# An audio-tower layer on one core: everything outside the attention loop re-laid with features on partitions and tokens on the free axis

## What is computed

```python
# 1. token mixing, x is [8, 4, 750]
a = x^T W1 + b1
for _ in range(8):
    up   = relu(a + shift_r(up)   @ W2.T + b2)
    down = relu(a + shift_l(down) @ W2.T + b2)
h = relu(x^T W3 + b3 + (shift_r(up) @ W4.T + b4) + (shift_l(down) @ W4.T + b4))
# 2. attention with L1 scores, 8 heads, x = layernorm(h)
q, vf, vb = split(x @ wqv.T + bias)
k = x * wk                                   # per head
a = softmax(-sum_w |q - k| / 8)              # with one more zero row
o = sum_heads(a applied to vf + a^T applied to vb)
h = h + x + (o * sigmoid(1.702 o)) @ fanin.T + fanin_b
# 3. mixture of 8 experts, the best 2 by score, x = layernorm(h)
share = softmax over the top 2 of (x @ Wg.T + bg), zero elsewhere
h = h + sum_e share_e * (relu(x @ W1_e.T + b1_e) @ W2_e.T + b2_e)
```

## Time and profile before

| | us |
|---|---|
| median of 3 runs | 9099.83 |
| lowest, highest | 9087.98, 9101.53 |
| the profiled execution | 9099.23 |
| its span, first to last instruction | 9097.4 |
| busy in it: PE, ACT, DVE, POOL | 8899.6, 7702.7, 7116.9, 96.7 |
| mean granted TensorE clock, share of full speed | 0.981 |

### The profile page before, as it was taken

The page is one execution under the profiler, slowest core; times in us unless marked ns, Lnnn a source line. Parts: engine busy times, 40 slices in busy tenths (PEclk is TensorE's granted clock), DMA queues, the critical chain, the costliest instruction groups (busy, mean ns, idle before and its releaser), DMA issues. The chain is left out here.

```text
span 9097.4 us, 256713 instructions
## 1 busy us (share of the span) xinstructions
PE 8899.6 (98%) x115498; PEld 7213.9 (79%) x115498; DVE 7116.9 (78%) x5443; ACT 7702.7 (85%) x3699; POOL 96.7 (1%) x90
## 2 busy tenths in 40 slices
PE   7699999999999999999999999999999999999979
PEld 4258996788858987889879897989856986897757
DVE  4688888888888888888888888888788888888843
ACT  2199999999999999999999999999999998999933
POOL 0000000000000000000000000000000000000021
PEclk7899999999999999999999999999999999999988
DMA  1510000001010100101000000001010000100000
GB/s 37 160 16 2 16 2 2 16 2 16 2 16 2 16 2 2 16 2 16 2 16 2 12 7 2 16 2 16 2 16 2 6 12 2 16 2 2 2 12 5
DMA packets 135450, 113.97 MB, mean 13 GB/s; under 512 B 111378, under 2 KB 115282, under 8 KB 134207
## 3 DMA queue, kind: packets, MB, share of 16 engines
q1 hardware_dynamic: 134366, 97.49, 5.3%
HBM read 57.23 MB, written 40.22 MB: 11 GB/s over the span
## 5 line engine op out<-in xcount | busy, mean ns | idle before, releaser
L676 PE MATMUL sc<-ring,window 128*32 128x375 f32 x96000 | 7973.8, 478 | 1.7 <-DVE ring L797 1.7
L727 ACT ACTIVATE ring<-qx,xs 128x3000 f32<-128x3000 f32 x2624 | 7178.8, 2792 | 726.5 <-PE sc L676 725.6
L797 DVE TENSOR_SCALAR ring<-qx,xs 128x3000 f32<-128x3000 f32 x3376 | 6132.5, 1837 | 1478.4 <-PE sc L676 1406.7
L676 PEld LDWEIGHTS sc<-ring,window 128*32 128x32 f32 x96000 | 6136.5, 109 | 1307.3 <-issue 354.4
L649 PEld LDWEIGHTS acc<-ext,vf 128*32 128x32 f32 x9408 | 366.2, 109 | 37.8 <-issue 9.1
L636 PE MATMUL acc<-ex,vb 128*32 128x375 f32 x3088 | 386.9, 478 | 1.5 <-DVE ex L754 1.5
L649 PE MATMUL acc<-ext,vf 128*32 128x128 f32 (+1 forms) x9408 | 378.0, 270 | 0.2 <-DVE ext L762 0.2
L762 DVE STREAM_TRANSPOSE ext<-ex 128x768 f32<-128x768 f32 x385 | 374.3, 972 | 0.6
L712 ACT ACTIVATE ex<-sc 128x750 f32<-128x750 f32 x385 | 298.9, 776 | 5.6 <-PE sc L676 5.6
L1088 ACT ACTIVATE hid<-pu,b1c 128x500 f32<-128x500 f32 x192 | 122.4, 677 | 210.6 <-PE pu L1052 210.6
L665 PE MATMUL sc<-ksum,select 128*32 128x375 bf16 x3072 | 265.1, 324 | 34.4 <-DMA vf<-scratch_v 18.3
(11 more groups left out here) (167 smaller groups left out, 1195.1 us busy)
## 6 DMA issues: line engine op xcount, KB each, us to landing
qx<-scratch_qk SPq DMA_DIRECT2D x64, 375.0 KB
scratch_v<-vs SPq DMA_DIRECT2D x38, 480.0 KB, 4.3
scratch_qk<-qs SPq DMA_DIRECT2D x32, 375.0 KB, 2.8
vb<-scratch_v SPq DMA_DIRECT2D x128, 92.0 KB
vf<-scratch_v SPq DMA_DIRECT2D x64, 184.0 KB
scratch_v<-w SPq DMA_DIRECT2D x12, 480.0 KB, 4.3
xs<-scratch_x SPq DMA_DIRECT2D x16, 187.5 KB
vb<-scratch_v SPq DMA_DIRECT2D x128, 1.8 KB
```

The source lines that it names most:

```text
L676: mm = pe.matmul(bank[32 * j:32 * j + 32, h, 0:HALF], window[:, HALF_NH * g + j, ROWS - 1 - i:3 * ROWS - 1 - i], ring[:, slot, j, h * HALF ...
L727: act.activation(flat(ring[:, (HALF * g + k) % RING, :, :]), flat(qx[g][:, :, :]), ACT.Abs, bias=xs[g][:, 1, k:k + 1], scale=0.5).then_inc ...
L797: vec.tensor_scalar(flat(ring[:, (HALF * g + k) % RING, :, :]), flat(qx[g][:, :, :]), xs[g][:, 0, k:k + 1], xs[g][:, 1, k:k + 1], ALU.max, ...
```

## The change

All of `phase_tokens` and `phase_feed` is rewritten; `phase_attend` is the same text. Everywhere a tensor is now [128, 3000]: 64 features of the first half of each clip on partitions 0 to 63, 64 features of the second half on 64 to 127. No tensor is turned between token mixing and the output.

- The mixing output uses the weights as stationary operand and 375 tokens as moving one, 32 matmuls for 96.
- Layernorm goes by chunks of 500 columns through PE, DVE and ACT: the mean of 64 partitions is a matmul with `avg`, the squares on ACT are summed by matmuls with `hsum`, the root's reciprocal is spread back over partitions by matmuls against `ident`. DVE, ACT and PE each run a loop over chunks in which the steps of several chunks alternate.
- The stationary and moving operands of q, v and `ups` have 64 rows, once for each half: six products of bf16 parts (`PRODUCTS`) for each of two halves, 12 matmuls where there were 6 for the same number of tokens. Neighbouring ones use rows 0 to 63 and rows 64 to 127 of the array and write different banks.
- q is written by ACT with bias and scale, into four buffers; v by DVE in chunks of 2x125 tokens, three buffers of 1 MB; per clip SP stores 4 tiles of q and then 3 of v. The sums `ks` come early; their splitting is on POOL.
- The weights of the second block are loaded and split during token mixing.
- `downs` has `w2t` stationary (128 rows, 64 columns, one half of the array's columns for each half of the tokens) and 500 columns of `hid` moving. The shares are brought onto all 64 partitions of a half by a matmul with `pick` (`shares`), copied by ACT, and DVE does (y + b2) * share and the sum, 500 columns at a time, two per expert and chunk.
- The top two are found by two passes of maximum and one-hot, in the first block of feed; `ups` of step n+1 is issued ahead of `downs` of step n, a step being two experts of a chunk (24 steps).
- Only the result is turned, 4 transposes per chunk (`turns`). `keep_warm` is gone.

```diff
@@ phase_tokens, first block, tensor
-                    for g in range(NC // 8):
-                        for k in range(8):
-                            c = 8 * g + k
-                            b, o = c // BC, 1 + CH * (c % BC)
-                            dst = ps[g // 2][0:CH, g % 2, D * k:D * k + D]
-                            pe.matmul(dst, last[:, b, o:o + CH], w4d[:, :], start=True, stop=False)
-                            mm = pe.matmul(dst, x7[:, CH * c:CH * c + CH], w3b[:, :], start=False, stop=True)
+                    for b in range(B):
+                        for h in range(2):
+                            pe.matmul(ps[b // 2][64 * h:64 * h + 64, b % 2, 0:HALF], w4d[:, :],
+                                      last[:, b, 1 + h * HALF:1 + (h + 1) * HALF], start=True, stop=False)
+                    for b in range(B):
+                        for h in range(2):
+                            mm = pe.matmul(ps[b // 2][64 * h:64 * h + 64, b % 2, 0:HALF], w3b[:, :],
+                                           x7[:, b * L + h * HALF:b * L + (h + 1) * HALF], start=False, stop=True)
@@ phase_tokens, second block, tensor
-                    keep_warm(pe, pv[0], oacc, 14)
+                    for c in range(NQC + 3):
+                        if c < NQC:
+                            mean(c)
+                        if 0 <= c - 2 < NQC:
+                            var(c - 2)
+                        if 0 <= c - 3 < NQC:
+                            spread(c - 3)
...
+                            for k, (i, j) in enumerate(PRODUCTS):
+                                for h in range(2):
+                                    mm = pe.matmul(pq[n % 2][:, h, 0:HALF], wp[i][64 * h:64 * h + 64, p * 128:(p + 1) * 128],
+                                                   xp[j][64 * h:64 * h + 64, b * HALF:(b + 1) * HALF],
+                                                   start=(k == 0), stop=(k == len(PRODUCTS) - 1))
@@ phase_tokens, second block, vector
+                    for c in range(NQC + 6):
+                        if c < NQC:
+                            center(c)
+                        if 0 <= c - 2 < NQC:
+                            invert(c - 2)
+                        if 0 <= c - 3 < NQC:
+                            normal(c - 3)
+                        if 0 <= c - 5 < NQC:
+                            rest(c - 5)
+                        if 0 <= c - 6 < NQC:
+                            third(c - 6)
@@ phase_feed, tensor
+                    def downs(n):
+
+                        first = n % NP * 2
+                        if n == 0:
+                            pe.wait_ge(w_down, 64)
+                        pe.wait_ge(relu_made, 4 * n + 4)
+                        for a in range(2):
+                            if n:
+                                pe.wait_ge(c_used, 2 * n - 1 + a)
+                            for u in range(2):
+                                for h in range(2):
+                                    mm = pe.matmul(pd[64 * h:64 * h + 64, a, 0:EC], w2t[:, first + a, u, :],
+                                                   hid[n % 2][:, a, u, h, :], start=(u == 0), stop=(u == 1))
...
+                    ups(0)
+                    turn_shares()
+                    for n in range(NI):
+                        if n + 1 < NI:
+                            ups(n + 1)
+                        shares(n)
+                        downs(n)
+                        if n % NP == 0 and n:
+                            turns(n // NP - 1)
+                    turns(NQC - 1)
```

More of the change, by code:

```diff
@@ L927, in _, with fan @@
[L927 to L932 removed]
+                    def fan(c):
+                        pe.wait_ge(g_made, c + 1)
+                        if c >= 2:
+                            pe.wait_ge(h_made, c - 1)
+                        pe.matmul(py[:, c % 2, 0:EC], fant[:, :], sg[:, cols(c)], start=True, stop=True).then_inc(y_sum, 1)
@@ new lines, in _ @@
+                    pe.wait_ge(w_first, 48)
+                    pe.wait_ge(eps_set, 3)
+                    pe.wait_ge(w_gate, 64)
+                    for c in range(NQC + 4):
+                        if c < NQC:
+                            fan(c)
+                        if 0 <= c - 1 < NQC:
+                            mean(c - 1)
+                        if 0 <= c - 3 < NQC:
+                            var(c - 3)
+                        if 0 <= c - 4 < NQC:
+                            spread(c - 4)
@@ new lines, in shares @@
+                    def shares(n):
+                        c, first = n // NP, n % NP * 2
+                        if n == 0:
+                            pe.wait_ge(w1_split, 5)
+                            pe.wait_ge(c_third, NQC)
+                        for a in range(2):
+                            if 2 * n + a >= 2:
+                                pe.wait_ge(c_kept, 2 * n + a - 1)
+                            if n % NP == 1 and n > NP and a == 0:
+                                pe.wait_ge(y_kept, n // NP)
+                            pe.matmul(pc[:, a, 0:EC], pick[:, first + a, :], cp[:, cols(c)], start=True, stop=True).then_inc(c_sum, 1)
@@ new lines, in _, with square, root @@
+                    for c in range(NQC):
+                        act.activation(sg[:, cols(c)], flat[:, cols(c)], ACT.Sigmoid, scale=1.702).then_inc(sg_made, 1)
+                    def square(c):
+                        act.wait_ge(cen_made, c + 1)
+                        act.activation(sq[:, cols(c)], cen[:, cols(c)], ACT.Square).then_inc(sq_made, 1)
+                    def root(c):
+                        act.wait_ge(var_sum, c + 1)
+                        act.activation(std[:, SUB * c:SUB * c + SUB, :], var_bank(c), ACT.Sqrt, bias=eps[0:CH, :]).then_inc(std_made, 1)
@@ new lines, in first, with second @@
+                    def first(c):
+                        act.wait_ge(x_made, c + 1)
+                        act.copy(xp[0][:, cols(c)], xt[:, cols(c)]).then_inc(x_first, 1)
+                    def second(c):
+                        act.wait_ge(x_left, c + 1)
+                        act.copy(xp[1][:, cols(c)], sq[:, cols(c)]).then_inc(x_second, 1)
+                    act.wait_ge(eps_set, 3)
+                    for c in range(NQC + 5):
+                        if c < NQC:
+                            square(c)
+                        if 0 <= c - 1 < NQC:
+                            root(c - 1)
+                        if 0 <= c - 4 < NQC:
+                            first(c - 4)
+                        if 0 <= c - 5 < NQC:
+                            second(c - 5)
@@ L945, in _ @@
+                    for n in range(NI):
+                        if n + 1 < NI:
+                            for g in range(4 * n + 4, 4 * n + 8):
+                                relu(g)
+                        keep(n)
+                        if n % NP == 0 and n:
+                            emit(n // NP - 1)
+                    emit(NQC - 1)
                 @block.vector
```

1178 lines of the change are left out of this document (620 added, 558 removed).

## The result

| | before | after |
|---|---|---|
| median (lowest, highest), us | 9100.68 (9087.98, 9104.02), 4 runs | 8947.69 (8944.07, 8950.86), 4 runs |
| ratio, 95% interval | | 0.9833 (0.982 to 0.9846) |
| the profiled execution | 9099.23 | 8950.86 |

The kernel got 153 us faster, 1.7%. Forecast were 268 us less, 8831, with a range to 8925: the time lies 22.7 us outside it.

The account below looks back on a forecast made before the run. PE was taken to bound attention's 8266.8 us, which stays; the other stages had mixed limits. From 9097.4, phase_tokens loses 135.8 and feed 132.3, giving 8829.3, plus 1.8 around the span: 8831 us, range 8770 to 8925.

Parts of the forecast that it names:

- stage 3: Stores of x, q and v in phase_tokens: DMA becomes the bound, 129 us for 210.1, bounds 121 and 137.
- The rivals: Three other outcomes: stores at q's pace 8917 (8%), halves not overlapping 9016 (7%), clock staying at half 9120 (3%).
- Stores stay at q's pace: Rival for the stores: gaps remain, 38.7 MB at 183 GB/s take 211 us, 86 more, total 8917; chance 8%.
- Attention: The attention loop between phase_tokens and feed: text unchanged, stays at 8267 us; moving by more than 5 would refute the cut.
- Mixing output and layernorm: Early phase_tokens: block with mixing output ends at 103.6 us, clock falling again; layernorm 25.4 for 39.7, first bulk store at 129.0.
- Feed loop: Feed's 24 steps: PE stays the bound at 9.6 us each, 230 us for 341.1, bounds 216 and 254.
- three changes of cut: Within each feed loop step: switching the PE array's tiling mode drains the engine, 0.6 us per step.
- Tail: End of the kernel after the feed loop: 7.5 us for 6.3.
- Feed's first block: Start of feed, pipeline, scoring and shares: 67 us for 89.4, bounds 56 and 87.
- What would show it: Signs listed: 9.6 us steps, feed-loop clock near 1.00, phase_tokens ending near 258 us, DMA share over 0.85, attention at 8267.

Follow-up runs that it names:

- e1_split112: The changed kernel with each 125-row v store issued as two, rows 0 to 111 and 112 to 124: 8845.06 us, ratio 0.9716 to the kernel before.

## Why the prediction was wrong, step by step

**The step that failed** is the sum of stage 3: "At 292/0.88 = 332 GB/s they need 117 us." Both numbers of the earlier trace rows were read rightly, but they belong to stores of 120 rows, and the change stores 125. The quotient took for granted that any store can use all 16 engines; v's could use 5. 24.6 MB at 131 GB/s are 188 us by themselves, q's pace comes on top, and the stage took 249.8 in place of 129: 120.8 us of an error that is 116.7 in all. With v cut in rows of 128 as far as they go, the stage took 129.2 and the kernel 8827, so the rest of the sum stood. That both came so near is partly luck. The stage ran faster in its middle than forecast (361 GB/s for 332) and lost some 6 us to POOL's addition, which I had not priced. The total has a stage that began 9.0 us early (119.95 for 129.0) and a feed some 3 us too long.

**The rivals** asked the right question about the wrong thing. "Stores stay at q's pace" (8917) looked at how many stores are in flight; the fourth buffer shows that at 125 rows their number didn't matter. Neither my bounds (121 to 137) nor the range took in a store that reaches fewer engines, although a new row count is a property of the change and stands in its diff. That the store stage would last longer than before, with less work on PE and DVE, was no case of mine.

**Attention** took 8266.2 us (8266.8 before), as said. **Mixing output and layernorm**: the block ended at 102.8 (forecast 103.6, though with the rounds 4.6 us later and the output 5.4 us shorter), the first bulk store was issued at 126.3 (129.0). The mechanism was off in both. I expected the clock to fall at the start of the output, and it held 0.99 until 98.6 us; and the layernorm's 23.5 us belong to a mean clock of 0.88, while in e1_split112, at 0.50, it took 34.6, over my bound of 31. These two terms came near by luck. **Feed loop**: 9.36 us per step for 9.6, 224.8 for 230. In it `ups` take 5.33 for 5.2, the shares 0.52 for 0.42 and `downs` 3.51 for 3.36, in all 0.51 more than the bare matmuls (5.07, 0.42, 3.36). The prediction had 0.6 for three changes of cut and 0.13 for a wait on top of them. How much of the 0.51 the changes of cut cost, no run separates; they don't stand between the terms as a gap of their own. The loads of the weights were read too short: 5.3/96 counts two records for each float32 load, so one took 0.11 us and not 0.055. The bf16 loads of the new loop take 0.08 (12 in 0.96 us) and stay hidden, so nothing hung on it. **Tail**: 7.6 for 7.5.

**Feed's first block**: 74.4 for 67. The pipeline's last `spread` came 51.1 us after attention's end for 41.5: the granted clock was 0.59 from 8661 to 8701 us, and DVE was held up by POOL. The scoring took 7.4 us for 8, DVE's part 12.5 for 10.4 and what follows it 3.4 for 7. With the gates moved, the holdup is gone and the stage takes 59.1 us (8643.7 to 8702.75), 8 less than the forecast. The prediction spoke of POOL's splitting only as work that hides; that it could hold up DVE meanwhile was priced nowhere.

**What would show it**, as listed: the loop's step, its clock (1.00) and attention's time came as forecast. "Phase_tokens ending near 258 us, DMA share over 0.85 in its last 125" was the one that failed (376.1, and 0.41 over the stage), and it pointed straight at the stage.

## What to carry to other kernels

A DMA rate read from a trace belongs to the shape it was measured with. Before it is applied to another tile, look at how many engines the new shape reaches: here 128, 120 or 112 rows ran at 354 to 405 GB/s, 125 at 131 and 127 at 26, so a store of an awkward number of rows is better cut in pieces with a large divisor of at most 16. And when a buffer wait is on the path, one more buffer is a cheap test of whether the wait is the cause or only where it shows; here the wait fell by two thirds and the time did not.

## What the runs showed of the hardware that was not expected

- For the eight row counts tried, the share of the DMA engines that a store from SBUF to DRAM keeps busy follows the largest divisor up to 16 of its row count: 405 GB/s for 128 rows, 26 for 127.
- A pair of stores, 112 and 13 rows, reached 291 GB/s at a share of 0.93, and 112 rows alone 354 at 1.00: busy engines are not all at the same pace. Why, is open.
- A DVE instruction with two inputs in SBUF stood 6.98 us for 0.67 while POOL's addition ran; an eviction from PSUM beside the same addition was not slowed (1.18 us).
- Six 64-row matmuls of one half issued ahead of the other half's cost 20.6 us, where a full loss of the overlap costs 120.8.
- The granted clock of 12 to 24 us is 0.50 before and 1.00 after, while a group of 16 matmuls of the rounds takes 2.78 us there in both and 1.49 later. At a start the clock is better read from durations.
